# Rotary attention: queries, keys and guard in bfloat16 thirds instead of float32r halves

## The reference, cut to what matters

```python
q_in = k_in = _apply_rope(layernorm(x));  v_in = layernorm(x)
q, k, v = q_in @ Wq.T + bq, k_in @ Wk.T + bk, v_in @ Wv.T + bv
scores = einsum('bqhd,bkhd->bhqk', q, k) / sqrt(8)      # masked to k <= q
attn = softmax(scores, axis=-1)
ctx = einsum('bhqk,bkhd->bqhd', attn, v)
x1 = _layer_norm(v_in + ctx @ out_proj_w.T + out_proj_b, ln1_w, ln1_b)
```

## Time and profile before

| | |
|---|---|
| median of 3 runs | 1835.31 us (1834.94 to 1835.55) |
| profiled execution, its own time | 1833.69 us |
| its span, first to last instruction | 1832.0 us |
| mean granted TensorE clock | 0.901 of 2.4 GHz |
| busy share of the span | PE 83%, PEld 53%, DVE 69%, ACT 56%, POOL 43% |
| rotary layer, first score to last product | about 386 to 774 us |

### The profile page before, as it was taken

One profiled execution on the slowest core, in us unless ns is written; L12 is line 12 of the kernel. 1 busy time (PEld: TensorE's weight loads), 2 busy tenths in 40 slices (PEclk: granted clock), 3 DMA queues, 4 the chain that ended last, 5 costly groups with the idle time before them and its releaser, 6 DMA issues. The chain is left out here.

```text
span 1832.0 us, 26742 instructions
## 1 busy us (share of the span) xinstructions
PE 1527.2 (83%) x8757; PEld 964.3 (53%) x8757; DVE 1262.7 (69%) x3220; ACT 1027.0 (56%) x1749; POOL 778.9 (43%) x894
## 2 busy tenths in 40 slices
PE   3788888379999999767859999999998587999980
PEld 1445555146666666433324555555553466777760
DVE  1656667467777777448777777777883565888875
ACT  2444554215666665524635766777676544777762
POOL 1133334344555554415652102222100476688875
PEclk8888889658999999969958999999999688999995
DMA  6600000132222221000154344443430022344415
GB/s 216 239 1 1 1 1 1 39 101 73 73 73 73 72 69 43 8 16 1 37 122 126 85 124 127 119 121 91 127 86 2 27 67 91 107 132 139 123 58 138
DMA packets 96201, 144.30 MB, mean 79 GB/s; under 512 B 31266, under 2 KB 59939, under 8 KB 91952
## 3 DMA queue, kind: packets, MB, share of 16 engines
q1 hardware_dynamic: 91072, 134.11, 26.3%
q0 software_dynamic: 4992, 8.48, 1.4%
HBM read 104.19 MB, written 57.48 MB: 88 GB/s over the span
## 5 line engine op out<-in xcount | busy, mean ns | idle before, releaser
L1068 DVE TENSOR_REDUCE ctx_nm<-ctx_s 128x1 f32<-128x512 f32 x496 | 319.8, 680 | 87.5 <-PE ctx_s L1202 86.7
L1068 DVE TENSOR_REDUCE rope_nm<-rope_s 128x1 f32<-128x128 f32 (+3 forms) x512 | 230.0, 480 | 85.2 <-PE rope_s L1205 82.7
L1479 ACT ACTIVATE rope_probs<-rope_st 128x1024 f32<-128x1024 f32 (+1 forms) x256 | 172.2, 702 | 138.4 <-PE rope_st L1587 137.2
L1479 ACT ACTIVATE ctx_probs<-ctx_st 128x1024 f32<-128x1024 f32 x192 | 190.3, 1022 | 88.9 <-PE ctx_st L1587 85.4
L1202 PE MATMUL ctx_s<-att_kst,att_qst 96*128 96x512 f32 x496 | 211.4, 460 | 18.3 <-PEq L120 7.7
L1202 PE MATMUL rope_s<-att_kst,att_qst 96*128 96x128 f32 (+3 forms) x512 | 184.8, 393 | 4.1 <-DVE rope_nm L1068 3.4
L1320 POOL TENSOR_SCALAR_AFFINE_SELECT rope_probs<-rope_probs 128x256 f32<-128x256 f32 x256 | 98.2, 408 | 169.9 <-ACT rope_probs L1479 169.4
L1587 PE MATMUL ctx_st<-att_qst,att_kst 98*128 98x512 f32 x512 | 164.5, 404 | 2.4 <-ACT ctx_probs L1479 1.5
L1202 PEld LDWEIGHTS ctx_s<-att_kst,att_qst 96*128 96x128 f32 x496 | 95.9, 193 | 126.6 <-DVE ctx_nm L1068 51.7
L1587 PE MATMUL rope_st<-att_qst,att_kst 98*128 98x512 f32 (+3 forms) x512 | 140.9, 359 | 3.9 <-ACT rope_probs L1479 3.9
L2865 DVE TENSOR_TENSOR sw_hl<-sw_hf,sw_hh 128x512 fp32r<-128x512 f32 x124 | 129.5, 1045 | 0.1
(11 more groups left out here) (411 smaller groups left out, 3445.0 us busy)
## 6 DMA issues: line engine op xcount, KB each, us to landing
sw_raw<-in_L_ffn_all SPq DMA_DIRECT2D x24, 768.0 KB, 4.5
sw_xs<-in_pad SPq DMA_DIRECT2D x65, 260.0 KB, 9.7
rope_halves<-att_qk SPq DMA_DIRECT2D x24, 512.0 KB
ctx_halves<-att_qk SPq DMA_DIRECT2D x24, 512.0 KB, 5.8
att_qst<-ctx_contexts SPq DMA_DIRECT2D x32, 384.0 KB
att_kst<-ctx_contexts SPq DMA_DIRECT2D x32, 384.0 KB
att_qst<-rope_halves SPq DMA_DIRECT2D x32, 192.0 KB
att_kst<-rope_halves SPq DMA_DIRECT2D x32, 192.0 KB
```

The costliest lines, as they stand in the source:

```text
L1068: nc.vector.tensor_reduce(nm[:, g, j * T + t:j * T + t + 1], bank("s", b, n)[:, 0:keys], AXX, ALU.max, negate=True).then_inc(s_used, 1)
L1479: nc.scalar.activation(prob(n // GH % 2, n % GH)[:, u * units[0]:u * units[0] + units[u]], st_bank[u][:, 0:units[u]], ACT.Exp, scale=SCALE ...
```

## The change

In the rotary layer alone, query, key and guard are held in bfloat16. Each of q and k is split into three bfloat16 parts, and six pairs of parts take 6 x 8 = 48 rows of the stack, in place of three pairs in 24 rows. The matmuls keep their rows (96 and 98), weights and columns, and now have bfloat16 operands. In detail:

- `halves_of` on POOL does four operations instead of two for each of q and k.
- `store_halves` issues six transfers instead of three; the bytes stay the same (12 parts of 2 bytes for 6 of 4). The loads of the stack stay two for a group, with twice the rows of half the length.
- `cut_guard` has four steps and five instructions on DVE instead of three: a cast to bfloat16 (`rounded`), a copy of it back to float32 and the subtraction, the transposition, and a cast of the transposed block to bfloat16 (`cutb`).
- The ones of `kst` are written as bfloat16 in `prepare`. Since the context layer still reads float32, POOL writes them again at the start of the mixture layer (`guard_of_ones`).
- The clearing of the stacks still goes over the whole float32 buffers.

The diff, cut to its core:

```diff
+    PAIRS, KIND = (6, BF16) if causal else (3, F32)
-    halves = nc.dram_tensor(layer + "halves", [B, 6, D, S], F32, kind="Internal").ap()
+    halves = nc.dram_tensor(layer + "halves", [B, 2 * PAIRS, D, S], KIND, kind="Internal").ap()
-    guards = nc.dram_tensor(layer + "guards", [NG, P, 32], F32, kind="Internal").ap()
+    guards = nc.dram_tensor(layer + "guards", [NG, P, 32], KIND, kind="Internal").ap()
-    NS = 48 if causal else 96
+    NS = 96
...
-        kst, qst, vaug, V = held.kst, held.qst, held.vaug, held.V
+        narrow = lambda ap: ap[:].rearrange("r g j s -> r (g j s)").bitcast(BF16)[:, 0:NG * GH * S].rearrange("r (g j s) -> r g j s", g=NG, j=GH)
+        kst, qst = (narrow(ap) if causal else ap for ap in (held.kst, held.qst))
+        thirds = qk4[:].bitcast(BF16).rearrange("p k (two s) -> p (k two) s", two=2)
...
             def store_halves(c):
                 sp.wait_ge(low_ready, c * 2 + 2)
-                copies(halves[c], qk4[:])
+                if causal:
+                    for k, part, n in ((0, 0, 3), (3, 1, 2), (5, 2, 2), (7, 3, 1), (8, 3, 2), (10, 4, 2)):
+                        sp.dma_start(halves[c, k:k + n].rearrange("k p s -> p k s"), thirds[:, part:part + n]).then_inc(stored, 16)
...
+                if causal:
+                    first, second, third = (thirds[:, n] for n in ((3, 4, 5) if k else (2, 1, 0)))
+                    ch.do(nc.gpsimd.tensor_copy(first, qk[:, k]))
+                    ch.sync()
+                    ch.do(nc.gpsimd.tensor_tensor(qk[:, k], qk[:, k], first, ALU.subtract))
+                    ch.sync()
+                    ch.do(nc.gpsimd.tensor_copy(second, qk[:, k]))
+                    ch.sync()
+                    nc.gpsimd.tensor_tensor(third, qk[:, k], second, ALU.subtract).then_inc(low_ready, 1)
+                    return
...
+            def guard_of_ones():
+                nc.gpsimd.memset(kst[KS:KM].bitcast(F32), 1.0).then_inc(init, 1)
+                pool.wait_ge(init, 1)
...
             def cut_guard(b, g, step):
+                if causal:
+                    if step == 0:
+                        dve.wait_ge(s_used, b * 64 + (g + 1) * GH * T)
+                        nc.vector.tensor_copy(rounded[:], nm[:, g]).then_inc(mh_ready, 1)
+                    if step == 1:
+                        dve.wait_ge(mh_ready, n + 1)
+                        if n:
+                            dve.wait_ge(turned_guard, n)
+                        nc.vector.tensor_copy(cut[:, 0], rounded[:]).then_inc(ml_ready, 1)
+                        nc.vector.tensor_tensor(cut[:, 1], nm[:, g], rounded[:], ALU.subtract).then_inc(ml_ready, 1)
+                    if step == 2:
+                        dve.wait_ge(ml_ready, 2 * n + 2)
+                        if n:
+                            dve.wait_ge(mT_ready, n)
+                        nc.vector.transpose(cutT[:], cut[:].rearrange("p h n -> p (h n)")).then_inc(turned_guard, 1)
+                    if step == 3:
+                        dve.wait_ge(turned_guard, n + 1)
+                        if n:
+                            dve.wait_ge(m_stored, n * 16)
+                        nc.vector.tensor_copy(cutb[:], cutT[:]).then_inc(mT_ready, 1)
+                    return
...
-                nc.gpsimd.memset(kst[KS:KM].bitcast(F32), 1.0).then_inc(init, 1)
+                nc.gpsimd.memset(kst[KS:KM], 1.0).then_inc(init, 1)
...
             nc.gpsimd.memset(half[:], -0.5).then_inc(half_ready, 1)
+            pool.wait_ge(half_ready, 1)
+            next_layer.guard_of_ones()
```

More of the change, by code:

```diff
@@ L783 @@
 SyncSteps = namedtuple("SyncSteps", "load_inputs store_halves load_stack fill_stacks store_guard load_guard")
-PoolSteps = namedtuple("PoolSteps", "inverse_root turn halves_of halves_of_context")
+PoolSteps = namedtuple("PoolSteps", "inverse_root turn halves_of halves_of_context guard_of_ones")
 VectorSteps = namedtuple("VectorSteps", "moments offsets rotate keep_values largest cut_guard")
@@ L854, in attention_layer @@
         at = lambda c: (units[0] if place[c][0] else 0) + place[c][1]
-        kst, qst, vaug, V = held.kst, held.qst, held.vaug, held.V
+        vaug, V = held.vaug, held.V
+        narrow = lambda ap: ap[:].rearrange("r g j s -> r (g j s)").bitcast(BF16)[:, 0:NG * GH * S].rearrange("r (g j s) -> r g j s", g=NG, j=GH)
+        kst, qst = (narrow(ap) if causal else ap for ap in (held.kst, held.qst))
+        as_stored = lambda ap: ap if causal else ap.bitcast(F32)
         by_slot = lambda ap: ap.rearrange("p (t d) -> p t d", t=T)
         nm = sb("nm", [P, NG, GH * T])
-        cut, cutT = sb("cut", [P, 2, GH * T], F32R), sb("cutT", [P, 32], F32R)
+        cut, cutT = sb("cut", [P, 2, GH * T], F32 if causal else F32R), sb("cutT", [P, 32], F32 if causal else F32R)
+        rounded, cutb = sb("rounded", [P, GH * T], BF16), sb("cutb", [P, 32], BF16)
         if causal:
@@ L947, in store_halves @@
                 sp.wait_ge(low_ready, c * 2 + 2)
-                copies(halves[c], qk4[:])
-                if not causal:
+                if causal:
+                    for k, part, n in ((0, 0, 3), (3, 1, 2), (5, 2, 2), (7, 3, 1), (8, 3, 2), (10, 4, 2)):
+                        sp.dma_start(halves[c, k:k + n].rearrange("k p s -> p k s"), thirds[:, part:part + n]).then_inc(stored, 16)
+                else:
+                    copies(halves[c], qk4[:])
                     sp.wait_ge(c_low, c * 2 + 2)
@@ L963, in store_guard @@
                 sp.wait_ge(mT_ready, b * NG + g + 1)
-                sp.dma_start(guards[g], cutT[:].bitcast(F32)).then_inc(m_stored, 16)
+                sp.dma_start(guards[g], cutb[:] if causal else cutT[:].bitcast(F32)).then_inc(m_stored, 16)
             def load_guard(b, g):
@@ L971, in load_guard @@
                     dst = qst[KS + part:KS + part + 1, g].rearrange("o j (t k i) -> o (j t) k i", t=T, i=32)
-                    sp.dma_start(dst.bitcast(F32), src).then_inc(m_loaded, 16)
+                    sp.dma_start(as_stored(dst), src).then_inc(m_loaded, 16)
             def load_inputs():
@@ L1275, in _ @@
             ch.start(0)
-            inverse_root, turn, halves_of, halves_of_context = on_pool(pool, ch)
+            inverse_root, turn, halves_of, halves_of_context, guard_of_ones = on_pool(pool, ch)
             if ALONE:
@@ L1582, in scores_by_key @@
                     pe.wait_ge(p_ready, n * 2 + u - 1)
-                elif u == 0 and causal:
+                elif u == 0:
                     pe.wait_ge(init, 1)
```

16 lines of the change are left out of this document (8 added, 8 removed).

## The result

The median after is 1813.32 us (1810.61 to 1818.72, four runs) beside 1835.43 us of the kernel before in the same series: ratio 0.9877, 95% interval 0.9847 to 0.9907. The forecast was 1806, the range 1788 to 1826. The profiled execution took 1810.61 us with a span of 1808.9, so 23.1 us of the span are gone, where 29.1 were forecast. The lines have moved: the score is L1249 (was L1202), the mask L1252 (L1205), the product by key L1634 (L1587), the reduction L1093 (L1068); the new guard steps are L1102, L1107 with L1108, L1113 and L1118.

The account below looks back on a forecast made before the run. The prediction took PE as the bound, busy 97% of a steady rotary batch, with DVE next. Main loop -33, start +1.5 and mixture fill +2.4 gave -29.1 us, so 1806 us, range 1788 to 1826.

Parts of the forecast that it names:

- the main loop: Rotary layer's eight batches: seven gain 4.6 us each, the eighth 0.8, together 33 us (11 to 46).
- Loads on PE: Rotary matmuls: faster bfloat16 weight loads cut exposed time from 0.45 to 0.10 us a head, 5.6 us a batch.
- the mask's 0.23 us after the 512-column score: Rotary head: start distance 0.02 us over streaming, read as the mask's exposed bfloat16 load; basis for 0.024 us a load.
- above all after each mask: Rotary head on PE: load time shows where the preceding matmul is shorter than the load, chiefly behind masks.
- I take 3.3: Rotary batch: DVE's remaining waits, 3.3 us beside 39.2 of work, giving a 42.5 us period.
- The DVE rival: Rotary batches: DVE takes over or most loads stay exposed, gain 2 to 3 us a batch, 1822 us; chance 0.22.
- The start: Start of the rotary layer: POOL's longer splitting is uncovered and costs 1.5 us, between 0 and 4.5.
- The bias cast: Mixture layer: POOL's fill of ones holds DVE's cast of the experts' biases, making the gates' chain 2.4 us late.
- this rival: PE's clock falls to its lower level because PE idles more; part of "something else", chance 0.04.

Follow-up runs that it names:

- the casts as reductions: The changed kernel with DVE's three guard casts done as reductions over an axis of one: 1824.54 us, 0.9851 of the kernel before.
- the control: The changed kernel itself run again, unaltered, as yardstick for the runs beside it: 1831.98 us, 0.9894 of the kernel before.
- no mask: The changed kernel without the mask's matmul behind each rotary score, the guard taken over future keys too: 1832.40 us, 0.9914 of the kernel before.
- POOL as before: The changed kernel with third parts of query and key left zero, so POOL splits in two operations, not four: 1843.04 us, 0.9938 of the kernel before.

## Why the prediction was near, and where it failed

The mechanism was right, and one term of the sum was too large: the main loop gave 22.3 us, not 33. Some luck brought the number closer. Of the 23.1 us, 3.0 lie in stretches that the change doesn't touch (1.1 ahead of the layer, 0.5 and 1.5 behind it), and the change itself is worth 20.1 where 29.1 were forecast.

- **Loads on PE: more than forecast.** I took 5.6 us a batch, with four of twelve loads of a head still exposed. By the median distances over 32 heads the four scores, four masks and four products by key of a head took 474 ns beyond streaming before and 64 after, so the true gain on PE is 6.6 us a batch, and 5 ns are left at each. The step that misled me is the reading of the mask's 0.23 us after the 512-column score as the mask's own load; the runs with the float32r mask show that it wasn't. Nor do the rows show the load "above all after each mask": before, the next matmul started 40 ns behind the mask's start, under the 53 of streaming, and the gap lay between a score and its mask and behind the products by key. The Trainium skill's 81 ns for a load and a 128-column matmul (TensorE: Matmul & The Clock Gate, Back-to-back issue gap) would have left 28 ns at each; the trace has 55 to 65 ns for such a pair.
- **"I take 3.3" for DVE's waits: the step that failed.** DVE waits for PE 6.4 us a batch, 7.2 with its other waits. PE's gain didn't turn into DVE's being the bound, but into both waiting, for each other and for ACT. DVE's busy time was forecast at 39.2 and is 37.1 (38.2 in the long batches): the casts and the subtraction last longer, as said (4.9 us a batch by their rows, 3.1 before), but overlap with the reductions more than I allowed. 39.2 + 3.3 = 42.5 was forecast, 37.1 + 7.2 = 44.3 came.
- **The DVE rival was partly true.** Casts held by POOL cost 0.7 us in a good batch (the casts as reductions), and a held subtraction or copy another 1.5 in a bad one (45.8 for 44.3). I had its collision but no price for it on the path, and not that its size changes from one execution to the next. Of the 1.8 us missing in a good batch (44.3 for 42.5) 0.7 are this. Halving the reductions, with the casts still held, gives 1.5, which can't be added to it; how the other 1.1 split between DVE's reductions, ACT and PE's own order isn't shown.
- **Edges.** The batches: the first gained 6.2 us (clock 0.90, was 0.82), the steady ones 2.8 to 3.0 and one 1.3, the seventh 2.5 (I gave it 4.6), the eighth 0.9 (0.8). The start: forecast 1.5 us later. By the time from the start of the program the first score is 0.3 us earlier and the first product by key 1.5, but POOL's first operation on q and k is 1.1 us earlier too, at the end of a layer that is the same. Counted from there the first store of the parts comes after 7.5 us instead of 4.9, the first score after 19.6 instead of 18.9, and the first product by key after 37.0 instead of 37.5: the longer splitting costs 0.8 us at the first score and is made up before the first batch. The bias cast: forecast +2.4, measured +2.7. From the mixture's gates to the end it is 1.5 us shorter, and 0.5 between the last value product and the bias cast; no run has a cause for either. The same code differs by as much between two profiles: 2.4 us in the one stretch (before, and with the float32r mask), 1.0 in the other (after, and the control).
- **The clock** stayed at 2.4 GHz in all steady batches of the change, but two experiments dropped it there, with work left out on PE (no mask) and with POOL as before; ahead of a fall PE was busy 2.33 of 3.50 us in the one and 1.47 of 3.30 in the other. The eighth batch, my evidence against this rival, has 1.00 before and 0.96 after. I had put the rival inside 0.04.

What stays open: what decides in an execution whether the second group's subtraction meets POOL's operation, and so whether its batches are mostly of 44.3 or of 45.8 us; whether the bad kind goes for good if the subtraction too has a form that isn't held; and the ACT side of the waits, which wasn't tried by itself.

## What to carry to other kernels

When the bounding engine gets faster, don't subtract its gain from the period: ask which waits between the engines stay, since those were hidden in its busy time. An operation that another engine holds up costs nothing while its engine has slack and comes onto the path with the change; choose a form that isn't held (here a reduction over an axis of one in place of a copy), look for the operation that is still held (here the subtraction), and keep long fills of POOL away from the next casts of DVE. The best version here is the change with these two, 0.9846 of the kernel before; its interval overlaps that of the change alone (0.9877), and its rotary layer took 341.8 us where that of the change took 346.1 and 352.0.

## What the runs showed of the hardware that was not expected

- A float32r score with its mask costs 13 to 100 ns beyond streaming, and a mask whose load takes twice as long leaves the steady batch at 47.16 us for 47.10. A bfloat16 score with its mask costs 9 to 16 ns: the two loads have rows of 99 and 101 ns, 200 together, and yet the matmul behind the mask starts 123 ns after the 128-column score. A load's duration is not what it costs.
- One subtraction of DVE on 128x16 that meets an operation of POOL (1.33 us in place of 0.16) goes with a batch that is 1.5 us longer.
- A fill by POOL, which reads nothing, held DVE's cast of 0.69 us for 2.7 us more.
- Leaving out PE work can lengthen the program: without 3.6 us of masks two batches grew from 44.3 to 47.7 us at a mean clock of 0.89.
